# Gated slots stage: the logarithm moved behind the exponentials of the older batches in ScalarE's program

## The reference

```
q, k, v = silu(x @ Wq.T), silu(x @ Wk.T), silu(x @ Wv.T)      # 4 heads of 32
f = log_sigmoid(x @ Wf.T) / 8 ;  s = 1 - exp(f) ;  gk = exp(f)
step1: S = S * gt + kt * st ;  ok = qt . S
qv = softmax(ok)
step2: S = S * gt + st * vt ;  ov = qv . S
o = silu(ov) ;  out = (o * rsqrt(mean(o*o) + EPS) * g_w) @ Wo.T
```

## Time and profile before

| | |
|---|---|
| median of 3 runs | 3883.62 us (3882.29 to 3890.34) |
| profiled execution: its time | 3877.61 us |
| profiled execution: its span | 3875.8 us |
| PE busy over the span | 3445.7 us (89%) |
| DVE busy | 2752.1 us (71%) |
| ACT busy | 2286.4 us (59%) |
| POOL busy | 2178.0 us (56%) |
| time from the first to the last SiLU of q (steps 1 to 16) | 2869.37 to 3179.4 us, 15 periods of 20.67 us in the mean |

### The profile page before, as it was taken

How to read it: one execution, slowest core, us unless ns; L and a number is a source line. 1 busy time by engine, 2 the same in 40 slices (tenths; PEclk the granted TensorE clock), 3 DMA queues, 4 the chain that set the end, 5 groups by cost and what they waited for, 6 DMA issues and landing times. The chain is left out here.

```text
span 3875.8 us, 89527 instructions
## 1 busy us (share of the span) xinstructions
PE 3445.7 (89%) x30494; PEld 2103.1 (54%) x30494; DVE 2752.1 (71%) x7221; ACT 2286.4 (59%) x5520; POOL 2178.0 (56%) x2263
## 2 busy tenths in 40 slices
PE   5999999996797999999999999996968886987578
PEld 1333333325693656665666566654946764765356
DVE  6888888867445778788888887874448884654565
ACT  2777777773334666666666666663347672864367
POOL 3333333316545778888887888875432332754275
PEclk9999999995797999999999999998979997997889
DMA  5443434312552222222222222223733331110001
GB/s 100 59 61 61 63 62 60 60 24 77 180 184 73 52 47 54 56 55 50 56 57 51 50 54 56 51 48 90 196 98 90 88 85 35 45 46 5 1 1 45
DMA packets 414451, 254.32 MB, mean 66 GB/s; under 512 B 251418, under 2 KB 340434, under 8 KB 412722
## 3 DMA queue, kind: packets, MB, share of 16 engines
q1 hardware_dynamic: 403316, 226.43, 25.8%
q0 software_dynamic: 10688, 22.17, 1.8%
HBM read 91.61 MB, written 45.94 MB: 35 GB/s over the span
## 5 line engine op out<-in xcount | busy, mean ns | idle before, releaser
L2774 POOL TENSOR_TENSOR ra_prob<-ra_prob,ra_inverse 128x256 f32<-128x256 f32 (+3 forms) x512 | 631.4, 1256 | 244.5 <-DVE ra_inverse L3101 243.2
L2563 DVE TENSOR_REDUCE ca_mx<-ca_ps_s 128x2 f32<-128x1024 f32 x512 | 600.6, 1211 | 120.3 <-PE ca_ps_s L2435 120.0
L3014 ACT ACTIVATE ra_prob<-ra_ps_s,ra_low 128x128 f32<-128x128 f32 (+3 forms) x1024 | 534.0, 532 | 229.4 <-DVE ra_low L3079 227.1
L2500 ACT ACTIVATE ca_pT<-ca_ps_p 128x512 f32<-128x512 f32 x1024 | 544.9, 600 | 204.4 <-PE ca_ps_p L2445 202.9
L3079 DVE CUSTOM_DVE_ANT_0 ra_ps_s<-ra_ps_s,ra_mask 128x128 f32<-128x128 f32 (+3 forms) x1024 | 479.8, 510 | 44.9 <-PE ra_ps_s L2954 44.6
L2435 PE MATMUL ca_ps_s<-ca_kst,ca_qst 128*128 128x512 bf16 x1024 | 392.4, 389 | 26.2 <-DMA ca_kst<-ca_bounce 12.6
L2445 PE MATMUL ca_ps_p<-ca_qst,ca_kst 128*128 128x512 bf16 x1024 | 386.5, 382 | 5.4 <-ACT ca_pT L2500 4.2
L3020 ACT COPY ra_probT<-ra_ps_t 128x512 f32<-128x512 f32 x384 | 227.1, 591 | 253.4 <-PE ra_ps_t L2855 253.4
L2855 PE MATMUL ra_ps_t<-ident,ra_prob 128*128 128x128 f32 x2560 | 350.0, 276 | 3.2 <-ACT ra_probT L3020 2.1
L2954 PE MATMUL ra_ps_s<-ra_kz,ra_qz 64*128 64x128 f32 (+3 forms) x2048 | 347.8, 458 | 4.8 <-DMA ra_kz<-ra_rot 3.9
L2767 POOL TENSOR_TENSOR ra_rot<-experts_second 128x512 f32<-128x512 f32 x256 | 327.6, 1301 | 40.7 <-DVE experts_second L3090 40.7
(11 more groups left out here) (492 smaller groups left out, 7259.9 us busy)
## 6 DMA issues: line engine op xcount, KB each, us to landing
ra_qz<-ra_rot SPq DMA_DIRECT2D x512, 64.0 KB
ra_kz<-ra_rot SPq DMA_DIRECT2D x512, 64.0 KB
moe_w_own<-moe_w1T SPq DMA_DIRECT2D x71, 256.0 KB
moe_w_own<-router_w SPq DMA_DIRECT2D x71, 256.0 KB
ca_kst<-ca_bounce SPq DMA_DIRECT2D x256, 64.0 KB
ca_bounce<-ca_thirds SPq DMA_DIRECT2D x192, 64.0 KB, 3.0
ca_qst<-ca_bounce SPq DMA_DIRECT2D x64, 192.0 KB
moe_hs<-moe_rows SPq DMA_DIRECT2D x71, 66.0 KB
```

The costliest lines, as they stand in the source:

```text
L2500: nc.scalar.activation(pT[:, (NS * hp + u) % PRING, :], ps_p[n % NP][:], ACT.Exp).then_inc(sg["drained"], 1)
L2563: nc.vector.tensor_reduce(mx[:, hm % 2, 2 * j:2 * j + 2], ps_s[m % 2][:].rearrange("p (b k) -> p b k", b=2), AX.X, ALU.max)\
L2774: nc.gpsimd.tensor_tensor(at, at, inverse[:, n % PROB, 2 * tile:2 * tile + 2].unsqueeze(2).broadcast_to([P, 2, keys]), ALU.mult)\
L3014: nc.scalar.activation(prob[:, n % PROB, tile, head, 0:keys], part(n, tile)[:, head, :], ACT.Exp, bias=low[:, n % PROB, at:at + 1], scale= ...
```

## The change

In ScalarE's `body` the logarithm (with its two waits) moves from behind the exponential of za to behind ex, the softmax exponential of i3, and ahead of oT, the SiLU of i4. Nothing else changes; no other engine's program is touched.

```
--- before.py
+++ after.py
@@ -1980,9 +1980,6 @@
                         nc.scalar.activation(za[:], ps_z[:], ACT.Abs).then_inc(sg["abs_done"], 1)
                         need(act, "abs_done", i1)
                         nc.scalar.activation(za[:], za[:], ACT.Exp, scale=-1.0).then_inc(sg["ze_done"], 1)
-                        need(act, "ze_done", i1)
-                        need(act, "f_done", i2)
-                        nc.scalar.activation(zl[:], za[:], ACT.Ln, bias=core.ones[:, 0:1]).then_inc(sg["log_done"], 1)
                     if live(i2):
                         need(act, "d_done", i2)
                         need(act, "b_done", i3)
@@ -1996,6 +1993,10 @@
                         need(act, "sub_done", i3)
                         need(act, "qv_done", i4)
                         nc.scalar.activation(ex[:], ok[:], ACT.Exp).then_inc(sg["ex_done"], 1)
+                    if live(i1):
+                        need(act, "ze_done", i1)
+                        need(act, "f_done", i2)
+                        nc.scalar.activation(zl[:], za[:], ACT.Ln, bias=core.ones[:, 0:1]).then_inc(sg["log_done"], 1)
                     if live(i4):
                         need(act, "o2_in", i4)
                         need(act, "y_in", i5)
```

## The result

The changed kernel takes 3902.6 us (median of 5, 3901.2 to 3904.5) against 3883.6 us: ratio 1.0047, 95% interval 1.0036 to 1.0059, so 14 to 23 us slower. The forecast was 3888.7 us with a range that ended at 3897. The table loads did go, 15 of them.

A forecast was written before the change was run, and what follows sets the result against it. No engine is full, so order within a step decides, with ScalarE's branch behind ex as new last wait: +8.0 us in twelve full steps, -2.9 in step 2, +5.1 on 3883.6 gives 3888.7 us, range 3881 to 3897.

The forecast's parts named there:

- what is ahead of ex: Full steps: exponentials start about 1.45 us earlier, but ex doesn't move as it waits for VectorE's ok; nothing won.
- the branch behind ex: Full steps: load, logarithm, load, oT, osq put ss 5.13 us after ex's end, 0.58 us later in step 12.
- step 2: Filling step, ScalarE's own chain: exponentials start 3.3 us earlier and xn starts earlier, -2.9 us.
- Step 3: Filling step: qv some 1 us earlier, xn 0.3 us later; counted as 0, bounds -0.9 and +0.3.
- what an undisturbed step grows by: Full step, with ss as last wait behind osq: grows by 0.58 us, to about 21.35 us.
- So the transposes of xn wait for TensorE alone: Behind ss: xn ends at about 3112.67, just before ss end (3112.85), so xn itself holds nothing up.
- After ss all is as before, so the step grows by 0.58 us.: Full steps, work behind the sums of squares: unchanged, so only the later ss adds, 0.58 us.
- 12 x 0.66: Steps 5 to 16: ss on average 0.66 us later per step behind ScalarE's branch, +8.0 us in all.
- late ex in every step: Rival: TensorE stalls make ex late, never made up; +14.5 us, 3898 us; 0.15 together with waiting row statistics.
- One table for both: Rival: one set holds exponential and logarithm, oT only 0.75 us later; -11 us, 3872 us; chance 0.04.

The follow-up runs named there:

- e9: Kernel before plus four dead copies between ex and oT, and two unread TensorE products ahead of the sums of squares: ratio 1.0042, 11 steps 238.7 us.
- e1: Kernel before plus four dead ScalarE copies (about 2.05 us) between ex and oT, nothing moved: ratio 1.0038, 11 steps 245.8 us.
- e2: Changed kernel plus two unread TensorE products (about 1.5 us) filling its wait ahead of the sums of squares: ratio 1.0022, 11 steps 240.6 us.
- e5: Kernel before with the logarithm moved only in the filling steps 1 to 3, old place from step 4 on: ratio 0.9996, 11 steps 235.6 us.
- filled kernels: Kernels with unread TensorE products put in its wait ahead of the sums of squares: e2 (1.0022), e9 (1.0042), and e7 (1.0034) with a second wait filled.
- e7: e2 plus one more unread 512-column product ahead of TensorE's wait for qv: ratio 1.0034, 11 steps 242.4 us.
- e8: Changed kernel with one table set for exponential and logarithm loaded by name ahead of za's exponential: ratio 0.9968, 11 steps 223.3 us.
- e4: Kernel before, logarithm left in place, with one table set for exponential and logarithm loaded by name: ratio 0.9974, 11 steps 225.9 us.
- e6: Kernel before plus two dead ScalarE copies (1.05 us) between ex and oT: ratio 0.9997, 11 steps 231.0 us.

## Why the prediction was wrong

- **Right: what is ahead of ex.** ex still starts 0.03 us after ok ends, 9.80 us into an undisturbed step in both kernels, and ScalarE's idle time before it grew from 0.5 to 2.0 us. 19 us of removed loads bought nothing there.
- **Right: the branch behind ex.** 5.12 us against 5.13; ss 0.53 us later in an undisturbed step, var and bT freed, the row statistics unharmed beside carry.
- **Right: step 2.** Its xn starts 9.40 us after the step's first SiLU and not 12.39: -3.0 for the forecast's -2.9. Step 3, counted as 0 with +0.3 as bound, grew by 0.7 to 1.1 us (clock 0.84 in place of 0.92), so that steps 1 to 4 together take 77.1, 75.5 and 75.4 us in the changed kernel's three profiles against 79.3 and 78.9.
- **Mis-sized: what an undisturbed step grows by.** 21.16 us in place of 20.77, +0.39 and not +0.58. The sum went by ss as the last wait. It isn't the last: the transposes of xn follow xn, not ss. How soon ss lets them start is seen in e9, where the filling makes ss last: 0.81 us after the start of ss, not 1.02. By that xn was last by 0.2 us before the change and is by 0.1 us after it, so ss moved by 0.53 us and the step by less. The prediction had xn's delay right, "3112.67 in place of 3112.23", 0.44 us for step 12, and that step grew from 20.73 to 21.16 us. "So the transposes of xn wait for TensorE alone" was the mistake.
- **The step that failed:** "After ss all is as before, so the step grows by 0.58 us." I had TensorE standing 1.6 us before every ss, and priced it as a wait alone. Behind it, in seven of eleven steps, comes a stretch at half speed, which the sum had at nothing. The seven low steps of the changed kernel's first profile take 23.55 us in the mean, 2.4 us more than the other four, 16.7 us together. 4.3 of these are late ex (0.65 to 1.14 us in five of them), and 12.4 us belong to the low clock: 1.4 to 1.7 us in six of the steps, 2.9 in step 11.
- **The size of the two parts.** As a step is the start of xn plus 6.4 us where nothing disturbs it, the eleven steps can be split at xn (us, sums over steps 5 to 15; the last column is what remains over 11 x 6.395):

| kernel | 11 steps | up to xn's start | behind it, beyond 6.395 each |
|---|---|---|---|
| before; second profile | 230.8; 230.5 | 159.1; 158.4 | 1.3; 1.8 |
| changed; second; third | 249.5; 248.4; 249.0 | 166.8; 166.8; 167.3 | 12.4; 11.2; 11.3 |
| e1 | 245.8 | 168.0 | 7.5 |
| e2 | 240.6 | 168.2 | 2.1 |
| e9 | 238.7 | 166.7 | 1.6 |
| e5 (order of before in these steps) | 235.6 | 159.2 | 6.1 |

The changed kernel's 18.7 us are 7.7 up to xn and 11.0 behind it. The forecast for these eleven steps was 12 x 0.66 = 7.9 less step 16's 5.13 - 4.44 = 0.7, 7.2 us: for the branch with its late ex that was right, though made from ss and not from xn. The 11.0 us, well over half of the loss, are the clock's. The filled kernels keep the first part and are rid of nearly all of the second. So within the eleven steps the cause is shown by three profiles of the changed kernel against e2, from one profile of e2; e7, with the wait filled too, also has one low step. e1 against e9 points the same way but is weaker: e1's 7.5 us behind xn are little more than e5's 6.1, which has the order of before there. In the median of the whole kernel only e2 shows it (1.0022 against 1.0047); e9 doesn't. The forecast of the whole, +5.1 us against +19.0 measured, is missed by 14, of which these 11 are the part that is explained; the rest lies in step 3, behind step 16 (2.5 us in the first profile) and in what the whole kernel moves by.
- **The rivals.** The slower one, late ex in every step, had the right sign and 14.5 of 19 us. Its mechanism is real, as in the changed kernel a late ex is never made up (step 14 of the second profile: ex 0.63 us late, the step 21.80 us, 0.64 over the undisturbed one), but it isn't in every step: five steps late by over 0.5 us in the changed kernel, four before. Most of the loss came by another way, so its nearness is luck. *One table for both* was worked out at -11 us; built as e8 it measured -12. The Trainium skill, "ScalarE: Activation LUTs", section "Table sets: the hidden batching unit", has one set with both functions and counts one load for a logarithm and an exponential; the trace of before had shown that it isn't chosen by itself, and e4 and e8 show two loads in a step, and a shorter time, when it is loaded by name.

What stays open: why the clock falls in one step and not in the next with the same waits, where the stalls within the small products come from, and where the filled kernels lose behind step 16. No run here tells that.

## What to carry to other kernels

An engine with slack ahead of one wait can have none behind it: follow moved work to the next thing that the same engine owes to others, here the SiLU, osq and TensorE's sums of squares, and xn. Find the last wait of a step by checking it over many steps: what ends it keeps its distance to the next step's start in all of them (xn, 6.39 to 6.41 us), and a near rival doesn't (ss, 5.59 to 5.74 us). Where the sum says that TensorE will stand still longer in every step, read the granted clock by stretches and price a step at the low level beside the wait itself. And before reordering around table changes, ask whether one set serves both functions: that took away two loads in a step and, in e8, 1.4 of the 2.05 us by which oT was late.

## What the runs showed of the hardware

- TensorE's clock fell from 1.00 to 0.50 after waits of 1.05 and 1.65 us with 1.7 us of work between them, and came back while it worked, after nearly 7 us here and after 3.4 us in the six other low steps of that profile. Nearly the same waits (1.04 and 1.64 us) left it at 1.00 in the neighbouring step. The order of before, too, had one, two and four low steps in three profiles (the third is e5, whose full steps are the same). A stretch of 3.4 us cost 1.3 to 1.7 us where it lay behind xn.
- A later osq can be a gain. In e6 it runs behind bT and not beside it, bT takes 0.68 us and not 1.53, so shift and with it xn come 0.63 us earlier, and undisturbed steps took 20.14 us against 20.77 before, though oT was 1 us later. In e4, where oT kept its place, the collision only moved on: the four-column shift took 1.00 us in place of 0.15.

```profile
2957.53 0.69 DVE L2153 TENSOR_TENSOR gsa_bT<-gsa_sT,gsa_ek 128x512 f32<-128x512 f32 x1
...
2957.85 1.27 POOL L2065 TENSOR_TENSOR gsa_osq<-gsa_oT 128x512 f32<-128x512 f32 x1 [0.95 <-ACT gsa_oT L2004]
...
2958.14 1.00 DVE L2157 SCALAR_TENSOR_TENSOR gsa_shift<-gsa_mv,gsa_rs 128x4 f32<-128x4 f32 x1
```

These are rows of e4's timeline, step 5. The Trainium skill, "SBUF — State Buffer", section "Who interferes with whom", calls the port pair that VectorE and GpSimd share an exclusive lock; that it is held for a whole instruction it says of VectorE's two-port modes. Here shift ends at 2959.14 us, 0.02 behind osq, and var in the earlier trace rows 0.04 behind carry, which agrees with a whole instruction. bT agrees only in part: it ends 0.55 us behind osq, less than the 0.68 it takes alone, and osq itself grew from 1.04 to 1.24 us. In e8 the logarithm's 0.72 us happen to move osq behind bT, and shift takes 0.15 us; its xn starts 0.97 us earlier than before (0.62 in e4), and its undisturbed steps take 19.7 to 19.9 us against e4's 19.9 to 20.2, although its oT comes later.
